# A pre-norm block of time mixing and a gated MLP: the two 1024x1024 layers by Strassen's scheme of seven block products

## What is computed

```
h  = layernorm(x)
xk, xv, xr = h * m + shift(h) * (1 - m), with m of their own   # shift: the token before
k, v = xk Wk, xv Wv;  r = sigmoid(xr Wr)                       # 256 -> 256
p, q = running log-max state and numerator over the tokens      # a scan in time
x  = x + (r * wkv(k, v, p, q)) Wo
g  = layernorm(x)
h  = silu(g W1 * s1) * (g W2 * s2)                              # 256 -> 1024
h  = gelu(h H1 * t1);  h = gelu(h H2 * t2)                      # 1024 -> 1024, twice
x  = x + h W3 * s3                                              # 1024 -> 256
```

## Time and profile before

| | |
|---|---|
| median of 3 runs | 1620.64 us |
| span of the profiled execution | 1618.0 us (the page gives no other time for it; the median of the runs is 2.6 above) |
| TensorE / VectorE / ScalarE / GpSimd busy | 1598.4 / 1063.5 / 772.3 / 213.3 us |
| TensorE in the chain that ended last | 96% |
| matmuls | 7150 |
| DMA | 29.71 MB, most of it in the first 40 us |

### The profile page before, as it was taken

The page is one execution under the profiler, slowest core; times in us unless marked ns, Lnnn a source line. Parts: engine busy times, 40 slices in busy tenths (PEclk is TensorE's granted clock), DMA queues, the critical chain, the costliest instruction groups (busy, mean ns, idle before and its releaser), DMA issues.

```text
span 1618.0 us, 19929 instructions
## 1 busy us (share of the span) xinstructions
PE 1598.4 (99%) x7150; PEld 1252.1 (77%) x7150; DVE 1063.5 (66%) x1936; ACT 772.3 (48%) x1144; POOL 213.3 (13%) x111
## 2 busy tenths in 40 slices
PE   7899999999999999999999999999999999999998
PEld 5578778787887878878787787878878787787887
DVE  8776675757758576675757767577675766767531
ACT  6553454535445354454535545354554534545342
POOL 2301020200202002020110202002020010202000
PEclk9799999999999999999999999999999999999999
DMA  8000000000000000000000000000000000000000
GB/s 329 14 1 1 26 0 26 0 23 3 0 26 0 26 0 0 26 0 26 0 6 19 0 26 0 26 0 0 26 0 26 0 0 26 0 26 0 13 1 13
DMA packets 18862, 29.71 MB, mean 18 GB/s; under 512 B 1312, under 2 KB 17824, under 8 KB 17824
## 3 DMA queue, kind: packets, MB, share of 16 engines
q1 hardware_dynamic: 18848, 29.52, 5.2%
HBM read 21.12 MB, written 8.39 MB: 18 GB/s over the span
## 4 chain that ended last, share of the span: by engine, by line
PE 96%; issue 0%; POOLq 0%; POOL 0%; DVE 0%; DVEq 0%
PE ffn L409 30%; PE ffn L412 29%; PE att L353 10%; PE ffn L396 4%; PE ffn L397 4%; PE att L396 4%; PE ffn L455 4%; PE att L397 4%; PE ffn L456 4%; PE att L362 3%; PE att L334 2%; POOLq L153 0%; POOL mix_v L949 0%; DVE mix_v L826 0%; DVEq L272 0%
## 5 line engine op out<-in xcount | busy, mean ns | idle before, releaser
L409 PE MATMUL ffn<-ha_hi,w_rnd 128*128 128x512 f32 x1024 | 413.1, 403 | 0.0
L409 PE MATMUL ffn<-hb_hi,w_rnd 128*128 128x512 f32 x1024 | 408.8, 399 | 0.0
L412 PE MATMUL ffn<-ha_lo,w_rnd 128*128 128x512 f32 x1024 | 403.3, 394 | 0.0
L412 PE MATMUL ffn<-hb_lo,w_rnd 128*128 128x512 f32 x1024 | 403.2, 394 | 0.0
L575 ACT ACTIVATE ha_hi<-ffn,vec 128x512 fp32r<-128x512 f32 x128 | 88.0, 687 | 353.1 <-PE ffn L412 353.1
L409 PEld LDWEIGHTS ffn<-ha_hi,w_rnd 128*128 128x128 f32 x1024 | 192.1, 188 | 49.9 <-issue 3.6
L412 PEld LDWEIGHTS ffn<-ha_lo,w_rnd 128*128 128x128 f32 x1024 | 192.0, 187 | 48.5 <-issue 3.6
L409 PEld LDWEIGHTS ffn<-hb_hi,w_rnd 128*128 128x128 f32 x1024 | 192.1, 188 | 47.5
L412 PEld LDWEIGHTS ffn<-hb_lo,w_rnd 128*128 128x128 f32 x1024 | 191.9, 187 | 45.9
L819 DVE TENSOR_TENSOR ha_lo<-ffn,ha_hi 128x512 fp32r<-128x512 f32 x128 | 85.5, 687 | 163.0 <-ACT ffn L577 163.0
L577 ACT ACTIVATE ffn<-ffn,vec 128x512 f32<-128x512 f32 x256 | 169.6, 662 | 8.4
(11 more groups left out here) (121 smaller groups left out, 2318.1 us busy)
## 6 DMA issues: line engine op xcount, KB each, us to landing
x_in<-in_x SPq DMA_DIRECT2D x32, 256.0 KB, 2.9
w_raw<-in_w_ffn SPq DMA_DIRECT2D x4, 2048.0 KB, 22.6
out<-mix_v SPq DMA_DIRECT2D x32, 256.0 KB, 2.2
w_raw<-in_w_ffn SPq DMA_DIRECT2D x3, 1024.0 KB, 11.5
wm<-in_w_mix SPq DMA_DIRECT2D x1, 1024.0 KB, 6.5
s_row<-in_s SPq DMA_DIRECT2D x1, 128.0 KB, 7.4
vec<-in_vectors SPq DMA_DIRECT2D x1, 21.0 KB, 5.2
```

The costliest lines, as they stand in the source:

```text
L409: pe.matmul(F[m % 4][:], w[:, c, m * P:(m + 1) * P], act(hi[:, c, :]), start=(c == 0), stop=False)
L412: mm = pe.matmul(F[m % 4][:], w[:, c, m * P:(m + 1) * P], act(lo[:, c, :]), start=False, stop=(c == HC - 1))
```

## The change

The activation of a hidden layer is cut in 2 x 2 blocks, of 512 features by 256 tokens (one sequence), and the weights in 2 x 2 blocks of 512 x 512. Seven products of blocks (steps 0 to 6) take the place of eight, in the variant with 15 additions. A step is 32 matmuls of 256 columns: 4 input chunks, 4 output chunks, rounded part and remainder.

- Activations: `blocks8` holds the four blocks B11, B12, B21, B22 and the differences T1 = B12 - B11, T2 = B22 - T1, T3 = B22 - B12, T4 = B21 - T2. VectorE makes the differences; ScalarE rounds the seven operands into `op_hi`, VectorE writes their remainders to `op_lo`, in operations of 512 to 2560 elements per partition. The gate's product is written to SBUF now, not back to PSUM.
- Results: the products accumulate in three PSUM areas X, Y, Z of 1024 elements. In between ScalarE copies the area to `parts` (after steps 0, 1 and 2) and VectorE adds PSUM and copy (`sum12` after step 3, `sum22` after step 4, `sum11` after step 5). C21 is what X holds after step 6. The Gelus are made once, of 256 elements each, to `blocks8`, 16 a layer.
- Weights: four sums S1 to S4 of weight blocks a layer are made once on GpSimd (operations of 2048 elements per partition), checked like the weights, and stored with the plain blocks to DRAM. In the loop each half step loads 512 KB into one of seven slots of `ring`; SyncE issues a load when TensorE has done a half step. H1 and H2 are no longer rounded by a cast.
- Newton steps of both norms go to GpSimd: twelve operations of 4 elements each time. The numerator waits for a later point (`dve_lo1` 5).
- The orders on all engines are new; the transposes of the second norm stand inside `last`, the projections in three groups between steps. The mixing half has two PSUM banks of its own, not four.

```diff
+        ring = sb("ring", [P, SLOTS, 2, 512], F32R)
...
+        parts = sb("parts", [P, 3, QC, SEG])
...
+        blocks8 = sb("blocks8", [P, 8, QC, SEG])
...
+        op_hi = sb("op_hi", [P, STEPS, QC, SEG], F32R)
+        op_lo = sb("op_lo", [P, STEPS, QC, SEG], F32R)
...
+        X = [acc0, acc2]
+        Y = [acc2, acc0]
+        Z = acc1
...
+        B11, T1, T2, B21, B22, T3, T4, B12 = range(8)
+        STEP_OPERAND = [B11, T1, T2, B22, T3, B21, T4]
+        FRESH = (0, 1, 5)
+        C11, C12, C22 = 0, 1, 2
...
+def load_ring(n):
+    l, s, h = n // (2 * STEPS), n // 2 % STEPS, n % 2
+    ld_ring[n % SLOTS].add(sp.dma_start(ring[:, n % SLOTS, :, :].rearrange("p c o -> p (c o)").bitcast(F32), scratch[l, s, h]))
+def refill(i, last=False):
+    for n in range(HALF_STEPS - SLOTS if last else HALF_STEPS):
+        pe_half.wait(sp, i, n + 1)
+        load_ring((n + SLOTS) % HALF_STEPS)
...
+    for k, (step, src) in enumerate(((S1_STEP, S1_), (S2_STEP, S2_), (S3_STEP, S3_), (S4_STEP, S4_))):
+        sp.wait_ge(sums[l], k + 1)
+        to_scratch(l, step, src[l], st_sums[l])
...
+    def step(i, l, s):
+        k = STEP_OPERAND[s]
+        fresh = s in FRESH
+        bank = (X[l], Z, X[l], Z, X[l], Y[l], X[l])[s]
+        for h in range(2):
+            n = 2 * STEPS * l + 2 * s + h
+            ld_ring[n % SLOTS].wait(pe, i, n // SLOTS + 1)
+            if l == 0 and s in (0, 2):
+                dve_lo.wait(pe, i, (1 if s == 0 else 3) + h)
+            if l == 1 and s in (0, 1):
+                dve_lo1.wait(pe, i, 2 * s + 1 + h)
+            if l == 1 and s in (3, 5, 6) and h == 0:
+                dve_lo1.wait(pe, i, {3: 5, 5: 6, 6: 7}[s])
+            for c in (2 * h, 2 * h + 1):
+                for m in range(QC):
+                    w = ring[:, n % SLOTS, c % 2, m * P:(m + 1) * P]
+                    out = bank[:, m * SEG:(m + 1) * SEG]
+                    pe.matmul(out, act(w), act(op_hi[:, k, c, :]), start=(fresh and c == 0 and m % 2 == 0), stop=False,
+                              skip_group_check=True)
+                    mm = pe.matmul(out, act(w), act(op_lo[:, k, c, :]), start=False, stop=(c == QC - 1), skip_group_check=True)
+            pe_half.add(mm)
+    def free(i, l, s):
+        if l == 0 and s == 0:
+            dve_prod.wait(pe, i, 5)
+        if l == 0 and s == 1:
+            dve_prod.wait(pe, i, 8)
+        if l == 1 and s == 0:
+            dve_c.wait(pe, i, 4)
+        if l == 1 and s == 5:
+            act_gelu[0].wait(pe, i)
+        if s in (2, 3, 4):
+            act_copy.wait(pe, i, 3 * l + s - 1)
+        if s == 6:
+            dve_c.wait(pe, i, 4 * l + 2)
+    def hidden(i, l, steps):
+        for s in steps:
+            free(i, l, s)
+            step(i, l, s)
...
+        dve_c.wait(pe, i, 5)
+        dve_lo2.wait(pe, i, 1)
+        accumulate(2, T1, 0, True)
+        accumulate(3, T1, 0, False)
+        dve_lo2.wait(pe, i, 2)
+        accumulate(2, B22, QC, False)
+        pe_w3.add(accumulate(3, B22, QC, False))
+        dve_lo2.wait(pe, i, 3)
+        accumulate(0, B11, 0, True)
+        accumulate(1, B11, 0, False)
+        if between:
+            between()
+        dve_lo2.wait(pe, i, 4)
+        accumulate(0, B21, QC, False)
+        pe_w3.add(accumulate(1, B21, QC, False))
...
     with pe.Fori(0, NT - 1) as i:
         gate(i)
-        hidden1(i, [0, 1, 2])
+        dve_prod.wait(pe, i, 7)
         transpose_x(WHOLE, i + 1)
-        hidden1(i, [3, 4])
-        project(WHOLE, i + 1)
-        hidden1(i, range(5, HC))
-        hidden2(i, range(5))
+        hidden(i, 0, [0, 1])
+        project(WHOLE, i + 1, [0, 1])
+        hidden(i, 0, [2])
+        project(WHOLE, i + 1, [2, 3])
+        hidden(i, 0, [3])
+        project(WHOLE, i + 1, [4, 5])
+        hidden(i, 0, [4, 5, 6])
+        hidden(i, 1, [0, 1, 2, 3, 4])
         project_out(WHOLE, i + 1)
-        hidden2(i, range(5, HC))
-        transpose_x2(WHOLE, i + 1)
-        last(i)
+        hidden(i, 1, [5, 6])
+        last(i, lambda: transpose_x2(WHOLE, i + 1))
     i = NT - 1
     gate(i)
-    hidden1(i, range(HC))
...
+def part(i, l, k, src, dst):
+    pe_half.wait(act, i, 2 * STEPS * l + 2 * k)
+    act_copy.add(act.activation(parts[:, dst, :, :], src[:].rearrange("p (m t) -> p m t", m=QC), ACT.Copy))
...
+def second_half(i):
+    gelu12(i, 0)
+    gelu22(i, 0)
+    for g in range(2):
+        gelu11(i, 0, g)
+        hi(i, B11, PAIR_OF[g], act_gelu[0], 2 * QC + 2 * g + 2, act_hi1)
+    for g in range(2):
+        hi(i, slice(T1, T2 + 1), PAIR_OF[g], dve_t1, 3 + g, act_hi1)
+    gelu21(i, 0)
+    hi(i, slice(B22, T3 + 1), ALL, dve_t1, 5, act_hi1)
+    part1(i, 1)
+    hi(i, B21, ALL, act_gelu[0], 4 * QC, act_hi1)
+    part5(i, 1)
+    part12(i, 1)
+    hi(i, T4, ALL, dve_t1, 6, act_hi1)
+    gelu12(i, 1)
+    round_out(i, 1, T1, B12)
+    gelu22(i, 1)
+    round_out(i, 2, B22, B22)
+    for g in range(2):
+        gelu11(i, 1, g)
+    round_out(i, 3, B11, B11)
+    gelu21(i, 1)
+    round_out(i, 4, B21, B21)
...
+    dst = blocks8[:, B11::B12 - B11, m, :] if m < QC else blocks8[:, B21:B22 + 1, m - QC, :]
+    dve_prod.add(dve.scalar_tensor_tensor(dst, by_half(PAIRS[m % 4][1]), s2[:, m:m + 1], by_half(mix_k[:, m % 2, :]),
+                                          ALU.mult, ALU.mult))
...
+def lo(i, ks, chunks, ready, k, done):
+    ready.wait(dve, i, k)
+    done.add(dve.tensor_tensor(op_lo[:, ks, chunks, :], blocks8[:, ks, chunks, :], op_hi[:, ks, chunks, :].bitcast(F32),
+                               ALU.subtract))
...
+def t234_gate(i, g):
+    dve_prod.wait(dve, i, QC + 2 * g + 2)
+    dve_t.wait(dve, i, g + 1)
+    chunks = PAIR_OF[g]
+    dve_t.add(dve.tensor_tensor(blocks8[:, T2::T3 - T2, chunks, :], blocks8[:, B22:B22 + 1, chunks, :].broadcast_to([P, 2, 2, SEG]),
+                                blocks8[:, T1::B12 - T1, chunks, :], ALU.subtract))
+    dve_t.wait(dve, i, 2 * g + 3)
+    dve_t.add(difference(T4, B21, T2, chunks))
...
+def sum12(i, l):
+    pe_half.wait(dve, i, 2 * STEPS * l + 8)
+    act_copy.wait(dve, i, 3 * l + 3)
+    dve_c.add(dve.tensor_tensor(parts[:, C12, :, :], by_chunk(Z), parts[:, C12, :, :], ALU.add))
+def sum22(i, l):
+    pe_half.wait(dve, i, 2 * STEPS * l + 10)
+    act_copy.wait(dve, i, 3 * l + 2)
+    dve_c.add(dve.tensor_tensor(parts[:, C22, :, :], by_chunk(X[l]), parts[:, C22, :, :], ALU.add))
+def sum11(i, l, g):
+    pe_half.wait(dve, i, 2 * STEPS * l + 12)
+    c = PAIR_OF[g]
+    dve_c.add(dve.tensor_tensor(parts[:, C11, c, :], by_chunk(Y[l])[:, c, :], parts[:, C11, c, :], ALU.add))
...
+def gate_early(i):
     prod(i, 0)
+    prod(i, 1)
+    t1_gate(i, 0)
+def gate_middle(i):
+    prod(i, 2)
+    lo01(i, 0)
+    prod(i, 3)
+    t1_gate(i, 1)
+    prod(i, 4)
+    lo01(i, 1)
+    prod(i, 5)
+    t234_gate(i, 0)
+    prod(i, 6)
+    lo26(i, 0)
+    prod(i, 7)
+def sums_hidden(i):
+    sum11(i, 0, 0)
+    sum11(i, 0, 1)
+    for g in range(2):
+        t1_hidden(i, g)
+        lo(i, B11, PAIR_OF[g], act_hi1, g + 1, dve_lo1)
+    for g in range(2):
+        t2_hidden(i, g)
+    for g in range(2):
+        lo(i, slice(T1, T2 + 1), PAIR_OF[g], act_hi1, g + 3, dve_lo1)
+    t3_hidden(i)
+    lo(i, slice(B22, T3 + 1), ALL, act_hi1, 5, dve_lo1)
+def rest_hidden(i):
+    lo(i, B21, ALL, act_hi1, 6, dve_lo1)
+    t4_hidden(i)
+    lo(i, T4, ALL, act_hi1, 7, dve_lo1)
+    sum12(i, 1)
+    lo_out(i, 1, T1, B12)
+    sum22(i, 1)
+    lo_out(i, 2, B22, B22)
+def outputs(i):
+    sum11(i, 1, 0)
+    sum11(i, 1, 1)
+    lo_out(i, 3, B11, B11)
 with dve.Fori(0, NT - 1) as i:
     t = i + 1
-    gate(i)
     ld_x.wait(dve, t)
     ln1_statistics(WHOLE, t)
-    reciprocal_deviation(WHOLE, t, WHOLE.blocks)
+    seed(WHOLE, t, WHOLE.blocks, dve_seed.add)
+    gate_early(i)
+    pool_rstd.wait(dve, i, 1)
     ln1(WHOLE, t)
-    lo1(i, 0)
-    lo1(i, 1)
-    lo1(i, 2)
-    mix(WHOLE, t)
-    lo1(i, 3)
-    lo1(i, 4)
+    gate_middle(i)
+    mix_difference(WHOLE, t)
+    mix(WHOLE, t, 0)
+    t234_gate(i, 1)
+    mix(WHOLE, t, 1)
+    lo26(i, 1)
+    mix(WHOLE, t, 2)
     running_max(WHOLE, t)
     exponents(WHOLE, t)
+    sum12(i, 0)
     recurrence(WHOLE, t)
-    lo1(i, 5)
+    sum22(i, 0)
     denominator(WHOLE, t)
-    for m in range(6, HC):
-        lo1(i, m)
+    sums_hidden(i)
     invert(WHOLE, t)
     weigh(WHOLE, t)
-    for m in range(5):
-        lo2(i, m)
+    rest_hidden(i)
     residual(WHOLE, t)
     ln2_statistics(WHOLE, t)
-    lo2(i, 5)
-    reciprocal_deviation(WHOLE, t, WHOLE.blocks)
+    seed(WHOLE, t, WHOLE.blocks, dve_seed.add)
+    outputs(i)
+    pool_rstd.wait(dve, i, 2)
     ln2(WHOLE, t)
-    for m in range(6, HC):
-        lo2(i, m)
+    lo_out(i, 4, B21, B21)
+    finish(i, 1, 1)
     rest_x2(WHOLE, t)
-    finish(i)
+    finish(i, 2, 0)
     WHOLE.dve_chain.end_tile()
...
+def newton_steps(s, t, k):
+    dve_seed.wait(pool, t - 1, k)
+    h, y, u = half_var[:], rstd[:], newton[:]
+    for step in range(NEWTON_STEPS):
```

(11 more changed lines are left out.)

513 lines of the change are left out of this document (305 added, 208 removed).

## The result

The changed kernel takes 1848.73 us (median of 4 runs, 1847.28 to 1851.44); the kernel before, run beside it, 1620.49 (4 runs, 1619.51 to 1621.17). The ratio is 1.141, 95% interval 1.139 to 1.143: 228 us slower. The profiled execution has a span of 1846.1 us. The forecast was 1782, the range 1705 to 1850.

What follows compares the result with a forecast made beforehand. A loop through VectorE's and ScalarE's ordered queues bounds the kernel: 91.1 us of TensorE plus 16.2 of waits make 107.3 a tile. Start-up 81 + 2.7 + 15 x 107.3 + last tile 86.2 gives span 1779.4, median 1782 us; range 1705 to 1850.

Steps and rivals of the forecast that it cites:

- rival 2: TensorE's clock falls in its waits in each tile: +1.5 to 4 us a tile, 1805 to 1842 us; chance 0.20.
- the ring: Weight loads in the tiles: forecast cost 0; as a rival, starved loads add 5 us a tile, 1820 us; chance 0.04.
- The rival that TensorE stays the bound: Tiles with 2 us of TensorE waits: 1563 us, faster; it decides from 96.5 us a tile, waits 5.4; chance 0.10.
- TensorE's term: Hidden layers' 448 matmuls of 256 columns at 0.1186 us take 53.1 us; TensorE needs 91.1 a tile, 6.6 less.
- last layer: TensorE waits 4.7 us a tile for the last layer's B11: 12.3 us of work against 7.6 of cover.
- the two `sum22`: TensorE's step 6 waits for VectorE's sum22 in both hidden layers: 1.8 us in layer 1, 2.4 in layer 2.
- PSUM copy: Layer 2's step 2 waits 1.4 us for the copy of its PSUM, behind four Gelus and the 2048-element rounding.
- layer 2's step 1: TensorE waits 0.4 us there for the step's remainder.
- The transposes: They wait 1.7 us for the seventh gate product: VectorE takes 16.6 us until then, the gate 14.9.
- the nine waits: All of TensorE's forecast waits in one tile, put at 16.2 us together; bounds 11.5 to 19.
- Three forecast waits: Layer 1: step 1 for the eighth product 0.7 us, step 2's second half for its remainder 0.8; layer 2's step 0: 2.2.
- The start-up term: Before the first tile: GpSimd's block sums at 5.5 us each, flag at 73.4, gate at 81 (range 74 to 90).

Runs made afterwards that it cites:

- Experiment 2: The changed kernel with VectorE's remainders made for 32 of 256 tokens, TensorE reading the rounded part twice: 1644.22 us.
- experiment 3: The changed kernel with each refill of the weight ring loading 256 KB instead of 512 KB: 1850.27 us.
- experiment 4: The changed kernel with only VectorE's order changed, product sums taken earlier, no instruction added or removed: 1764.04 us.
- experiment 10: The changed kernel with remainders for 32 of 256 tokens, VectorE's product sums taken earlier, and two filling matmuls before layer 2's step 0: 1607.64 us.
- experiment 6: The changed kernel with each of GpSimd's block sums in 8 instructions of 256 elements instead of one of 2048: 1850.17 us.

## Why the prediction was right, and where it missed

**The number: inside the range by 1.3 us.** The range ended at 1850; the forecast's own 1705 to 1810 and rival 2's 1805 to 1842 both lie below the measured 1848.7, and the gate's start lies outside its bounds of 74 to 90. Two terms were too small, the tiles by 60 us and the start-up by 11.7, and that both together still fitted is luck. The direction and the mechanism are not.

**The sign and the cause: right.** The forecast was that 6.6 us of columns buy a loop through three queues that is longer than TensorE's work. Experiment 2 shows that VectorE's added time makes it so, experiment 3 excludes the ring, and experiment 4 shows that the order of VectorE's queue counts beside its total: 5.5 us a tile with the same instructions, 13.3 with a fifth less time on VectorE and the old order. No run shortens ScalarE's part of the loop, so its share stays open; with both edits (experiment 10) 95.5 us a tile are left against TensorE's 90.2 and two filling matmuls. The rival that TensorE stays the bound took waits of 2 us a tile and a turning point at 5.4; there were 13.3.

**TensorE's term: right.** 0.1167 us for 256 columns with the stationary operand from the ring, 52.3 us for the 448 against 53.1. The estimate of 98 ns a matmul of 256 columns (on the straight line between the two figures) from the Trainium skill ("TensorE: Matmul & The Clock Gate", "Back-to-back issue gap") isn't borne out here: in these matmuls the distance is nearly proportional to the columns, 0.1167 for 256 and 0.2334 for 512.

**The waits: nearly right.** In the waits shown above, forecast against measured: last layer 4.7 and 4.72 (3.2 to 3.4 in nine of fifteen tiles, see the result), the two `sum22` 1.8 and 1.94, 2.4 and 2.45, PSUM copy 1.4 and 1.12, layer 2's step 1 0.4 and 0.42. The transposes waited 3.1 instead of 1.7: normalising stood 1.76 us behind Newton steps that I had put at 0.2 apart instead of 0.28 (1.0 us for the twelve), and they are on the path. (Two small slips of the prediction: layer 1's step 6 is 9.2 - 7.6 = 1.6, entered as 1.8, and the nine waits add to 16.1.) Three forecast waits weren't there (0.7 and 0.8 in layer 1, 2.2 at step 0 of layer 2); the last is covered by the matmuls of the step before, which run at the lower clock. In the three tiles where the clock stayed up there, it is 1.5; experiment 4, which has no wait ahead of those matmuls, has it at 3.0.

**The failed step: the forecast's own clock and the start-up.** The sum took a clock of 1.00 in the tiles and left its fall to rival 2, at 0.20, for +1.5 to 4 a tile. It fell after 49 of 59 waits of 1.9 to 4.7 us. A tile has 7.8 us that the forecast didn't (6.3 by the clock, 1.5 unassigned), of which 2.9 are offset by shorter waits and 0.9 by the columns: 107.3 + 7.8 - 2.9 - 0.9 = 111.3. Rival 2 had the mechanism and, with 1805 to 1842, most of the size. The row was there: 5.23 us of idling followed by a clock of 0.50, beside waits of 4.7 and 2.4 that I had forecast myself. A mechanism that the trace shows once, and that the forecast repeats 16 times, belongs in the sum.

**The start-up term** was mis-sized by 11.7 us: gate at 92.7, not 81. The step read "GpSimd adds four 2048-element blocks at ... 5.5" and followed GpSimd's queue alone. The sums took 4.8 each, less than I had assumed; what I left out is that VectorE is held for the whole of one. The second sequence's exponentials began at 44.8, where with short sums they began at 29.8, three instructions before the second weighing (L955, L957 and L968, 57.87 to 71.81) lost 3.4 to 4.2 us each, and the flag came at 84.8 instead of 73.4. GpSimd waited for VectorE in its turn, 6.48 us before its numerator, so that its last sum ended at 76.2 and not at 70.5. The trace of before had a small case of it that I didn't use: between the rows of GpSimd's start-up numerator, at 29.50, VectorE's two-element copy (L753) took 1.12 us, and ended with GpSimd's instruction:

```profile
29.50 1.12 DVE L753 COPY seq<-carry_q 128x2 f32<-128x2 f32 x1
```

The Trainium skill has the rule in "SBUF — State Buffer", "SBUF: two separate sides": a VectorE instruction in a 2-port perf mode, or with two SBUF inputs beside a GpSimd instruction that reads SBUF, needs the pair of ports that the two engines share; whichever starts first has it for its whole instruction, and the other is blocked. By that rule the rest of GpSimd's instruction is the price, and the trace agrees, with 4.50 to 4.89 beside sums of 4.8, and with the reciprocals of one input that were not held; experiment 6 agrees too, with 0.69 beside instructions of 256 elements.

## What to carry to other kernels

An edit that takes columns off a saturated TensorE and gives work to an engine at two thirds of the span must be walked through the queues: busy shares allowed it, and even taking the columns away for nothing brought only two thirds of their price. Where the walk shows waits of 2 us and more on TensorE, add the clock to the sum: here TensorE lost 6.3 us a tile by it beside waits of 13.3, of which about half came off the waits again and at least 2.3 was net. And before a long GpSimd instruction is put beside VectorE's small ones, count its whole length once for each copy, tensor_scalar or two-input instruction of VectorE that may meet it, the kinds that were held here; splitting it frees VectorE and makes GpSimd's work longer (52.0 for 38.2 us).

## What the runs showed of the hardware

- After a wait of 1.9 us TensorE's clock fell, 1.5 us after the work had begun again (matmuls 0.12 apart until 484.2, then 0.21). After the waits of 2.45, 3.1 and 4.7 shown above it was low from the first matmul on (256 columns in 0.58 us, not 0.39). Waits of the same length had other outcomes in other tiles: of 59 between 1.9 and 4.7 us, ten were followed by no fall.
- VectorE's two-element copy took 4.50 us beside a 2048-element tensor_tensor of GpSimd, 0.69 beside one of 256 elements and 0.16 alone. Two reciprocals of 256 elements took 3.35 beside such a sum and 3.36 without.
- GpSimd's sums took 36% longer in eight parts (52.0 against 38.2 us); pieces of 256 elements followed each other at 0.68 us with VectorE idle, 5.6 for eight, where one instruction of 2048 took as little as 4.54.
- A GpSimd tensor_tensor of 4 elements per partition takes 0.20 us, and dependent ones follow each other at 0.28.
- A ring that moves 141 GB/s through a tile, in loads of 512 KB, made no wait and cost no time that one run could show.
